# P turned inside one tile, six blocks moved, and the splits of P cut by key block

## The chip, the core and the metric

The kernel runs on one core of a Trainium2 chip. The metric is device time in microseconds of one execution. The core has TensorE (PE in the profile, with its weight loads as PEld), VectorE (DVE), ScalarE (ACT), GpSimd (POOL) and SyncE (SP, which here only issues DMAs; SPq is its queue, and ACTq is ScalarE's). Sixteen DMA engines move the data.

## What is computed

The reference, cut to what matters:

```python
x = x + einsum('bct,bcd->bdt', x, w0[idx])          # 32 batches, 128 x 1024, w0[idx] is 128 x 128
q, k, v = (einsum('bsd,ed->bse', x, W) for W in (Wq, Wk, Wv))   # 16 heads of 64
scores = einsum('bhqd,bhkd->bhqk', q * min(cond, 4), k) / sqrt(64)
scores = where(causal, scores, most negative)
attn = softmax(scores)                               # 128 queries x 128 keys per head
x = x + einsum('bsd,ed->bse', einsum('bhqk,bhkd->bhqd', attn, v), Wo)
```

All of it is float32. The kernel splits each operand of a product into a high half that TensorE takes in its fp32r form and a low half, the rest, and multiplies high by high, low by high and high by low into the same bank.

## The kernel before

The batches are taken in 8 groups of four. The program has three parts: the per-batch 128x128 product with the values projection (up to about 400 us), the attention with the q and k projections (400 to 1275 us), and the output projection (the first group in eight blocks inside the end of the attention part, the other 28 batches as 14 pairs behind it). The products of the values and of the pairs are seven block products in place of eight, with sums of blocks made on GpSimd.

The attention part is made of **cells**, numbered n = 0 to 63. One cell is four of the group's batches by two heads. In a cell TensorE runs eight steps of the q projection and eight of k (each step three 128x512 matmuls), the scores of an earlier cell (L710 to L712 into SC) and the values of a still earlier one. The written order is a table of times: each piece of work has a due time in units of TensorE steps, a cell is 16 of them, and each engine walks the times in quarter steps. A due time sets only the order on an engine; semaphores do the rest.

What happens to P, the softmax's numerator, in cell n (a is five steps behind the cell's key block):

- VectorE masks the scores (L1205) and takes row maxima (L1211), ScalarE makes the exponential with its row sums (L1035), VectorE the reciprocals (L1215), GpSimd the normalised P in two halves of 128x512 (L1333). PP holds it: query rows, then batch, head, key column.
- VectorE turns each 32x32 block of a half where it stands (L1102, `dve_turn`), into the tile TB, or WR from cell 58. The block of query block i and key block j then lies in the rows of i; TensorE needs it in the rows of j.
- SyncE moves the ten blocks of the lower triangle (L1530, `sp_move_p`), 32 rows by 256 elements each, from TB to the tile of P: PT in even cells, PT2 or xr[1] in odd ones. The masked blocks of these tiles are zeroed once.
- ScalarE makes the high half of two batches at a time (L1045), a 128x512 piece per half cell P = 2n + k, and GpSimd the low half (L1336). Both go to the tile PS, of which there is one.
- TensorE multiplies the values by PS: four matmuls 128x256 for each P (L815). Cell n's splits and values run while the projections of two cells later run. A values group waits for the low half of its own half cell.
- ScalarE and VectorE take the result from the two PV banks (L1052, L1053 into AC, and L1229 into AT), GpSimd adds them (L1339), SyncE stores (L1656).

Other work stands between: the splits of weight pieces in 48 of the cells (ScalarE L1012 or L1068, VectorE L1186 or L1235, SyncE's stores L1443 and L1445 or those of `sp_store_wo`), the splits of the group's values (L999, L1327), and in the last cells the split of the first output group's attention (Y: L1057 on ScalarE, L1343 on GpSimd).

Near the end of the attention SyncE's queue also has the loads of x1 for the eight output blocks (L1511), their stores (L1680), the loads of Wo (L1571; four further ones on ScalarE's queue, L965, behind the last splits of P), the loads of the first pairs' attention (L1586, which for the first pair wait for the last split of P) and those of the pairs' x1 (L1598, which wait for all eight output stores). VectorE gathers the pairs' products into x1 (L1261) and makes the low halves of their operands (L1239); GpSimd adds parts of the products to x1 (L1377) and makes the sums of blocks, the first of which is L1359.

## Time and profile before

| what | value |
|---|---|
| three runs | 1571.53, 1571.56, 1573.22 us (median 1571.56) |
| the profiled execution | 1573.44 us |
| its span, first to last instruction | 1572.10 us |
| PE busy | 1560.5 us (99%) |
| DVE, ACT, POOL busy | 980.2 (62%), 818.6 (52%), 856.7 us (54%) |
| mean granted TensorE clock | 0.999 |
| DMA traffic | 341.46 MB, mean 217 GB/s |
| GpSimd's low halves of P, L1336 | 128 of 128x512, 1293 ns each |
| ScalarE's high halves of P, L1045 | 128 of 128x512, about 620 ns each |
| moves of P, L1530 | 640 of 32 KB |

TensorE's busy time is near the span, so what the other engines do matters only where TensorE waits for it. A row of the waits says which engine waited, the tile and line it was about to work on, who released it, the total, how often, and the longest. A row of the timeline has the start, the time taken, the engine, its line, the operation with tiles, and in brackets the idle time before it.

### The profile page before, as it was taken

Reading aid. Unit: us, or ns where it says so; the run is one execution under the profiler, and the core shown is the slowest. Engines: PE = TensorE matmul, PEld = TensorE weight load, DVE = VectorE, ACT = ScalarE, POOL = GpSimd, SP = SyncE. Lnnn points to the kernel's source line nnn. Section 1 sums busy time; section 2 is a strip of 40 time slices with the busy share of each in tenths; the row PEclk is TensorE's granted clock in tenths of the full one; section 3 lists DMA queues with packets and bytes.
Section 4 is the critical chain, followed back from the end, with each engine's and each line's share of the span. In section 5 each row is a group of like instructions: output and inputs, shape, how many; then the busy total and the mean of one; then the engine's idle time right before and its main releaser. Section 6 shows DMA issues by size and latency. Waiting matters only on the chain.

```text
span 1572.1 us, 23424 instructions
## 1 busy us (share of the span) xinstructions
PE 1560.5 (99%) x7563; PEld 1311.5 (83%) x7563; DVE 980.2 (62%) x1748; ACT 818.6 (52%) x2221; POOL 856.7 (54%) x752
## 2 busy tenths in 40 slices
PE   9999999999999999999999999999999998999999
PEld 7888888888888888888888888888888876888887
DVE  5844454443367777777766777777777654555553
ACT  6645545543366666666666666666666621222220
POOL 1545645643255566557655566675577544555552
PEclk9999999999999999999999999999999999999999
DMA  9958888865866666767677466666665696444442
GB/s 325 338 209 276 306 285 296 300 218 217 304 184 193 208 204 201 209 193 193 184 241 235 154 176 209 192 189 194 192 180 154 232 353 240 167 161 164 164 162 86
DMA packets 192299, 341.46 MB, mean 217 GB/s; under 512 B 23986, under 2 KB 116402, under 8 KB 185010
## 3 DMA queue, kind: packets, MB, share of 16 engines
q1 hardware_dynamic: 191026, 331.59, 65.6%
q10 hardware_dynamic: 1152, 8.39, 1.3%
q8 instruction: 60, 0.98, 0.3%
q14 instruction: 61, 0.50, 0.1%
HBM read 184.70 MB, written 134.22 MB: 203 GB/s over the span
## 4 chain that ended last, share of the span: by engine, by line
PE 95%; DMA 3%; SPq 1%; POOL 0%; DVE 0%; issue 0%; ACT 0%; DVEq 0%; POOLq 0%; ACTq 0%
PE p_PJ L710 22%; PE p_PJ L711 22%; PE p_PJ L712 22%; PE p_SC L710 6%; PE p_SC L712 6%; PE p_SC L711 6%; PE p_PV L815 4%; PE p_PV L710 1%; PE p_PV L712 1%; PE p_PV L711 1%; DMA out<-t_LATE 1%; PE p_LP L710 1%; PE p_LP L712 1%; PE p_LP L711 1%; DMA t_LATE<-x_scratch 1%; PE p_PV L841 1%
## 5 line engine op out<-in xcount | busy, mean ns | idle before, releaser
L711 PE MATMUL p_PJ<-t_XL,t_WH 128*128 128x512 f32 x1008 | 394.1, 391 | 0.0
L710 PE MATMUL p_PJ<-t_XH,t_WH 128*128 128x512 f32 x1008 | 394.1, 391 | 0.0
L712 PE MATMUL p_PJ<-t_XH,t_WL 128*128 128x512 f32 x1008 | 392.1, 389 | 0.0
L1035 ACT ACTIVATE t_PP<-t_PP,t_st 128x128 f32<-128x128 f32 x512 | 199.5, 391 | 174.5 <-DVE t_st L1211 173.0
L1333 POOL TENSOR_TENSOR t_PP<-t_PP,t_st 128x512 f32<-128x512 f32 x128 | 133.4, 1042 | 204.9 <-DVE t_st L1215 204.9
L712 PEld LDWEIGHTS p_PJ<-t_XH,t_WL 128*128 128x128 f32 x1008 | 189.3, 188 | 40.4
L710 PEld LDWEIGHTS p_PJ<-t_XH,t_WH 128*128 128x128 f32 x1008 | 190.0, 189 | 33.8
L711 PEld LDWEIGHTS p_PJ<-t_XL,t_WH 128*128 128x128 f32 x1008 | 190.0, 188 | 32.3
L1229 DVE TENSOR_REDUCE t_AT<-p_PV 64x256 f32<-64x512 f32 x252 | 171.2, 680 | 20.8 <-ACT t_AC L1053 12.0
L1339 POOL TENSOR_TENSOR t_AT<-t_AT,t_AC 128x256 f32<-128x256 f32 x126 | 117.2, 930 | 122.7 <-DVE t_AT L1229 122.7
L1336 POOL TENSOR_TENSOR t_PS<-t_PT,t_PS 128x512 fp32r<-128x512 f32 x122 | 157.8, 1293 | 0.0
L1205 DVE SCALAR_TENSOR_TENSOR t_PP<-p_SC,t_beta,t_mask 128x256 f32<-128x256 f32 x256 | 111.6, 477 | 44.2 <-PE p_SC L712 44.2
L1322 POOL TENSOR_TENSOR t_xl<-t_XT,t_xh 128x512 fp32r<-128x512 f32 x56 | 74.0, 1321 | 94.9 <-ACT t_xh L917 94.2
L1215 DVE RECIPROCAL t_st<-t_st 128x4 f32<-128x4 f32 x128 | 22.9, 179 | 142.0 <-ACT t_PP L1035 142.0
L1022 ACT ACTIVATE t_KH<-p_PJ 64x512 fp32r<-64x512 f32 x128 | 76.1, 594 | 48.2 <-PE p_PJ L712 46.5
L1052 ACT ACTIVATE t_AC<-p_PV 64x256 f32<-64x256 f32 x128 | 48.9, 382 | 93.8 <-PE p_PV L815 92.3
L1035 ACT ACTIVATION_READ_ACCUMULATOR t_PP<-t_PP,t_st 128x1 f32 x512 | 95.6, 187 | 0.0
L1327 POOL TENSOR_TENSOR t_VV<-t_VX,t_VV 128x512 fp32r<-128x512 f32 x64 | 81.4, 1293 | 25.9 <-ACT t_VV L999 25.9
L1192 DVE TENSOR_TENSOR t_KL<-p_PJ,t_KH 64x512 fp32r<-64x512 f32 x128 | 88.2, 689 | 11.0 <-ACT t_KH L1022 7.1
L1211 DVE TENSOR_REDUCE t_st<-t_PP 128x2 f32<-128x256 f32 x256 | 94.1, 409 | 0.0
L815 PE MATMUL p_PV<-t_PS,t_VV 128*128 128x256 f32 x512 | 82.0, 283 | 1.2 <-POOL t_PS L1336 0.8
L815 PEld LDWEIGHTS p_PV<-t_PS,t_VV 128*128 128x128 f32 x512 | 74.2, 190 | 7.0 <-POOL t_PS L1336 1.2
(254 smaller groups left out, 3547.9 us busy)
## 6 DMA issues: line engine op xcount, KB each, us to landing
t_XH<-xth_scratch SPq DMA_DIRECT2D x56, 512.0 KB, 6.6
t_XL<-xtl_scratch SPq DMA_DIRECT2D x56, 512.0 KB, 7.0
t_PT<-t_TB SPq DMA_DIRECT2D x580, 32.0 KB, 2.4
v_scratch<-t_VR SPq DMA_DIRECT2D x64, 256.0 KB, 4.4
xth_scratch<-t_XH SPq DMA_DIRECT2D x16, 1024.0 KB, 4.0
xtl_scratch<-t_XL SPq DMA_DIRECT2D x16, 1024.0 KB, 6.3
t_VX<-v_scratch SPq DMA_DIRECT2D x32, 512.0 KB, 5.6
at_scratch<-t_AT SPq DMA_DIRECT2D x126, 128.0 KB, 3.4
```

What stands on the lines that cost most here:

```text
L710: pe.matmul(bank, lh, rh, start=first, stop=False, skip_group_check=goes_on)
L711: pe.matmul(bank, lh, rl, start=False, stop=False, skip_group_check=goes_on)
L712: return pe.matmul(bank, ll, rh, start=False, stop=last, skip_group_check=goes_on)
L815: mm = pe.matmul(PV2[:, z, 256 * h:256 * h + 256], VV[j % 2][:, u, 2 * c + h, :], moving, start=True, stop=True)
L1035: act.activation(PP[:, u, h, :], PP[:, u, h, :], ACT.Exp, bias=st[:, 0, u, h:h + 1], scale=1.0, accum_out=st[:, 1, u, h:h + 1]).then_inc(a ...
L1192: dve.tensor_tensor(KL[r, :, k], pj[r], KH[r, :, k].bitcast(f32), ALU.subtract).then_inc(dve_k, 1)
L1205: dve.scalar_tensor_tensor(out=PP[:, u], in0=SC[u // 2][:, 256 * (u % 2):256 * (u % 2) + 256].rearrange("p (h k) -> p h k", h=2), scalar=b ...
L1211: dve.tensor_reduce(st[:, 0, u, :], PP[:, u], AX, ALU.max, negate=True).then_inc(dve_m, 1)
L1229: dve.tensor_reduce(at_tile(P)[r], both, AX, ALU.add).then_inc(dve_M, 1)
L1333: pool.tensor_tensor(pp, pp, r, ALU.mult).then_inc(pool_n, 1)
L1336: pool.tensor_tensor(p_half(P, 1), p_raw(P), p_half(P, 0).bitcast(f32), ALU.subtract).then_inc(pool_pt, 1)
L1339: pool.tensor_tensor(at_tile(P), at_tile(P), AC[:, P % 2], ALU.add).then_inc(pool_at, 1)
```

## The change

Turned blocks are written straight into the tile of P (TB or PT2 before cell 58, PT or WR from there). The four blocks on the diagonal are then in their place already. Six DMAs move the others, from the lower to the upper triangle of the same tile. Each parity of cells has its own semaphore for them. What the moves leave behind in the lower triangle is no longer zero, so the splits read, for key blocks of one query block i, only the rows up to 32i + 31: four splits per cell and engine, each of all eight batch-heads of the cell, on 32, 64, 96 and 128 rows with 256 elements in a row. The rows that they never write are zero in PS, which is filled once instead of the tiles of P. The due times of the splits and of the moves change, and the values groups wait for all four splits of their cell.

```diff
-                move_at.put(a + 10, n)
+                move_at.put(a + 10.5, n)
...
-                    half_at.put(a + (20 if last else 25.25) + 0.5 * k, P)
-                    ptl_at.put(a + (20.75 if last else 26) + 1.5 * k, P)
+                    if k == 0:
+                        half_at.put(a + (18 if last else 22.25), n)
+                        ptl_at.put(a + (18.75 if last else 23.25), n)
...
-        def turned(n):
-
-            return TB[:] if n < 58 else WR[:].rearrange("p a (b c) -> p (a b) c", b=2).rearrange("p j (u q) -> p j u q", u=8)
-
         def p_tile(n):
 
-            return PT if n % 2 == 0 else PT2 if n < 58 else xr[1][:].rearrange("p (i q) -> p i q", i=4)
+
+            if n < 58:
+                return TB[:] if n % 2 == 0 else PT2[:].rearrange("p j (u q) -> p j u q", u=8)
+            if n % 2 == 0:
+                return PT[:].rearrange("p j (u q) -> p j u q", u=8)
+            return WR[:].rearrange("p a (b c) -> p (a b) c", b=2).rearrange("p j (u q) -> p j u q", u=8)
...
-        def p_half(P, low):
-
-            u = 4 * (P % 2)
-            return PS[:, u:u + 4, low, :].rearrange("p u (i q) -> p u i q", i=4)
-
-        def p_raw(P):
-            u = 4 * (P % 2)
-            return p_tile(P // 2)[:].rearrange("p i (u q) -> p u i q", u=8)[:, u:u + 4]
+        def p_half(i, low):
+
+            return PS[0:32 * i + 32, :, low, 32 * i:32 * i + 32]
+
+        def p_raw(n, i):
+            return p_tile(n)[0:32 * i + 32, i]
...
-                pe.wait_ge(pool_pt, P + 1)
+                pe.wait_ge(pool_pt, 4 * n + 4)
...
-                for P in half_at(tick):
-                    n = P // 2
-                    act.wait_ge(l_P, 160 * (n + 1))
+                for n in half_at(tick):
+                    act.wait_ge(l_P[n % 2], 96 * (n // 2 + 1))
+                    act.wait_ge(dve_t, 2 * n + 2)
                     if n:
                         act.wait_ge(pe_pv, 4 * n)
-                    act.activation(p_half(P, 0), p_raw(P), ACT.Copy).then_inc(act_pt, 1)
+                    else:
+                        act.wait_ge(pool_z, 4)
+                    for i in range(4):
+                        act.activation(p_half(i, 0), p_raw(n, i), ACT.Copy).then_inc(act_pt, 1)
...
-            elif n == 58:
-                dve.wait_ge(s_O, 32 * 32)
-            elif k == 0:
-                dve.wait_ge(l_P, 160 * n)
+            elif n >= 2 and k == 0:
+
+                dve.wait_ge(pool_pt, 4 * (n - 1))
...
-                    pool.memset(PT[:], 0.0).then_inc(pool_z, 1)
-                    pool.wait_ge(dve_g, 5 * (NP - 2))
-                    pool.memset(PT2[:], 0.0).then_inc(pool_z, 1)
-                if tick == (T_END - 76) * TICK:
-                    pool.wait_ge(dve_O, 32)
-                    pool.memset(xr[1][:], 0.0).then_inc(pool_z, 1)
+                    pool.memset(PS[:].bitcast(f32), 0.0).then_inc(pool_z, 1)
...
-                for P in ptl_at(tick):
-                    pool.wait_ge(act_pt, P + 1)
-                    pool.tensor_tensor(p_half(P, 1), p_raw(P), p_half(P, 0).bitcast(f32), ALU.subtract).then_inc(pool_pt, 1)
+                for n in ptl_at(tick):
+                    for i in range(4):
+                        pool.wait_ge(act_pt, 4 * n + i + 1)
+                        pool.tensor_tensor(p_half(i, 1), p_raw(n, i), p_half(i, 0).bitcast(f32), ALU.subtract).then_inc(pool_pt, 1)
...
             sp.wait_ge(dve_t, 2 * n + 2)
-            if n == 0:
-                sp.wait_ge(pool_z, 5)
-            elif n >= 2:
-                sp.wait_ge(pool_pt, 2 * n - 2)
-            if n == 59:
-                sp.wait_ge(pool_z, 6)
+            tile = p_tile(n).rearrange("p j u q -> p j (u q)")
             for i in range(4):
-                for j in range(i + 1):
-                    src = turned(n)[32 * i:32 * i + 32, j].rearrange("a u q -> a (u q)")
-                    sp.dma_start(p_tile(n)[32 * j:32 * j + 32, i, :], src).then_inc(l_P, 16)
+                for j in range(i):
+                    sp.dma_start(tile[32 * j:32 * j + 32, i], tile[32 * i:32 * i + 32, j]).then_inc(l_P[n % 2], 16)
```

Waits elsewhere that counted the half cells' splits (the loads of Wo and of the first pair, the first sum of a pair) count the new ones to the same point.

How it moves the order on three queues. First GpSimd, in one cell of the middle of the attention, from its two normalising operations (t_PP) on; t_PS are the splits, t_AT the sums, t_VV the split of values. Before:

```order
L1333 TENSOR_TENSOR t_PP<-t_PP,t_st 128x512 x2
L1336 TENSOR_TENSOR t_PS<-t_PT,t_PS 128x4x128
L1339 TENSOR_TENSOR t_AT<-t_AT,t_AC 128x256
L1336 TENSOR_TENSOR t_PS<-t_PT,t_PS 128x4x128
L1327 TENSOR_TENSOR t_VV<-t_VX,t_VV 128x4x128 x2
L1339 TENSOR_TENSOR t_AT<-t_AT,t_AC 128x256
```

And with the change, in the same cell:

```order
L1331 TENSOR_TENSOR t_PP<-t_PP,t_st 128x512 x2
L1335 TENSOR_TENSOR t_PS<-t_PT,t_PS 32x8x32
L1335 TENSOR_TENSOR t_PS<-t_PT,t_PS 64x8x32
L1335 TENSOR_TENSOR t_PS<-t_PT,t_PS 96x8x32
L1335 TENSOR_TENSOR t_PS<-t_PT,t_PS 128x8x32
L1338 TENSOR_TENSOR t_AT<-t_AT,t_AC 128x256
L1325 TENSOR_TENSOR t_VV<-t_VX,t_VV 128x4x128 x2
L1338 TENSOR_TENSOR t_AT<-t_AT,t_AC 128x256
```

The second split of a cell stood behind a sum of AT; all four now stand ahead of it.

Next SyncE's queue in an early cell that also splits a weight piece; t_VX is the load of values, t_OH and t_OL the halves of the weight piece. Before:

```order
L1656 DMA at_scratch<-t_AT 128x256
L1499 DMA t_VX<-v_scratch 128x1024 x2
L1530 DMA t_PT<-t_TB 32x256 x10
L1443 DMA wh_scratch<-t_OH 512x1x128
L1445 DMA wl_scratch<-t_OL 512x1x128
L1656 DMA at_scratch<-t_AT 128x256
```

With the change:

```order
L1649 DMA at_scratch<-t_AT 128x256
L1498 DMA t_VX<-v_scratch 128x1024 x2
L1442 DMA wh_scratch<-t_OH 512x1x128
L1444 DMA wl_scratch<-t_OL 512x1x128
L1523 DMA t_TB<-t_TB 32x256 x6
L1649 DMA at_scratch<-t_AT 128x256
```

The two stores of the weight piece's halves stand ahead of the moves now.

Last, SyncE's queue around the last cell's moves; t_LATE and t_xr hold x1 and the output. Before:

```order
L1571 DMA t_WL<-wol_scratch 128x2048
L1511 DMA t_LATE<-x_scratch 128x512
L1511 DMA t_xr<-x_scratch 128x512
L1530 DMA t_xr<-t_WR 32x256 x10
L1680 DMA out<-t_xr 128x512
L1656 DMA at_scratch<-t_AT 128x256
L1511 DMA t_xr<-x_scratch 128x512
```

With the change:

```order
L1564 DMA t_WL<-wol_scratch 128x2048
L1510 DMA t_LATE<-x_scratch 128x512
L1510 DMA t_xr<-x_scratch 128x512
L1523 DMA t_WR<-t_WR 32x256 x6
L1673 DMA out<-t_xr 128x512
L1649 DMA at_scratch<-t_AT 128x256
L1510 DMA t_xr<-x_scratch 128x512
```

The order stays; six DMAs stand where ten stood.

## Rows read from the trace of the kernel before

**Rows 1.** Windows: stretch, its length, each engine busy (instructions), clock, DMA share, GB/s.

```profile
420.00:740.00 320.00, 320.00 (x1631) 273.52 (x1630) 233.83 (x474) 205.83 (x644) 188.17 (x169) 1.00 0.69 200
```

**Rows 2.** Waits of PE from 1240 to 1345: total, times, longest.

```profile
PE p_SC L710 <- DVE t_xr L1261: 2.0, 1, 2.0
PE p_SC L710 <- issue: 1.8, 1, 1.8
PE p_SC L710 <- DVE t_XL L1239: 1.0, 1, 1.0
```

**Rows 3.** Windows, two of 2 us behind the last of these waits.

```profile
1317.00:1319.00 2.00, 2.00 (x7) 1.58 (x8) 0.46 (x1) 0.00 (x0) 1.05 (x1) 0.72 0.69 258
1319.00:1321.00 2.00, 2.00 (x6) 1.59 (x5) 0.00 (x0) 0.00 (x0) 1.50 (x2) 0.50 0.10 35
```

**Rows 4.** Timeline of an ordinary cell: start, time taken, engine, line, operation.

```profile
870.46 1.14 ACT L1045 ACTIVATE t_PS<-t_PT 128x512 fp32r<-128x512 f32 x2
...
871.37 1.30 POOL L1336 TENSOR_TENSOR t_PS<-t_PT,t_PS 128x512 fp32r<-128x512 f32 x1
...
873.86 0.73 POOL L1339 TENSOR_TENSOR t_AT<-t_AT,t_AC 128x256 f32<-128x256 f32 x1 [1.20 <-DVE t_AT L1229]
...
874.28 0.65 PEld L815 LDWEIGHTS p_PV<-t_PS,t_VV 128*128 128x128 f32 x4
874.51 0.64 PE L815 MATMUL p_PV<-t_PS,t_VV 128*128 128x256 f32 x4
874.56 1.28 POOL L1336 TENSOR_TENSOR t_PS<-t_PT,t_PS 128x512 fp32r<-128x512 f32 x1
```

**Rows 5.** Timeline of the last ordinary cell, n = 61.

```profile
1244.52 1.30 POOL L1336 TENSOR_TENSOR t_PS<-t_xr,t_PS 128x512 fp32r<-128x512 f32 x1
...
1247.43 0.65 PEld L815 LDWEIGHTS p_PV<-t_PS,t_VV 128*128 128x128 f32 x4
```

**Rows 6.** Timeline of a cell with the split of a weight piece.

```profile
604.83 1.30 POOL L1336 TENSOR_TENSOR t_PS<-t_PT,t_PS 128x512 fp32r<-128x512 f32 x1
...
607.28 0.69 DVE L1186 TENSOR_TENSOR t_OL<-t_xr,t_OH 128x512 fp32r<-128x512 f32 x1
607.33 1.24 POOL L1339 TENSOR_TENSOR t_AT<-t_AT,t_AC 128x256 f32<-128x256 f32 x1 [1.20 <-DVE t_AT L1229]
```

**Rows 7.** Timelines of POOL and DVE where the pairs' operands begin.

```profile
1281.38 1.30 POOL L1359 TENSOR_TENSOR t_WR<-t_PP,t_PT 128x512 f32<-128x512 f32 x1 [5.10 <-DMA t_PT<-at_scratch]
...
1282.00 1.23 DVE L1239 TENSOR_TENSOR t_VL<-t_PP,t_VH 128x512 fp32r<-128x512 f32 x1 [3.41 <-ACT t_VH L1080]
```

**Rows 8.** Timeline of SyncE's queue at the last cell's moves: time taken is that of issue.

```profile
1259.28 6.24 SPq L1530 DMA_DIRECT2D t_xr<-t_WR  x10
1265.57 0.58 SPq L1680 DMA_DIRECT2D out<-t_xr  x1
...
1273.67 0.38 SPq L1586 DMA_DIRECT2D t_PP<-at_scratch  x1
```

**Rows 9.** Page, DMA issues: count, KB each, median us from issue to landing.

```profile
t_PT<-t_TB SPq DMA_DIRECT2D x580, 32.0 KB, 2.4
```

**Rows 10.** Timelines of POOL and PEld in cell 59.

```profile
1218.37 1.29 POOL L1336 TENSOR_TENSOR t_PS<-t_xr,t_PS 128x512 fp32r<-128x512 f32 x1
...
1220.78 0.65 PEld L815 LDWEIGHTS p_PV<-t_PS,t_VV 128*128 128x128 f32 x4
```

**Rows 11.** Windows around the end of the attention; the last two numbers are DMA share and GB/s.

```profile
1266.00:1270.00 4.00, 4.00 (x19) 3.30 (x19) 1.28 (x3) 1.15 (x2) 0.00 (x0) 1.00 0.55 154
...
1274.00:1302.00 28.00, 27.65 (x124) 22.70 (x123) 14.51 (x18) 8.71 (x17) 12.10 (x9) 1.00 1.04 402
```

**Rows 12.** The chain that ended last, from 1240 to 1345: start, time taken, what.

```profile
1284.43 15.57 DMA t_LATE<-x_scratch
...
1316.17 0.70 DVE t_xr L1261
```

**Rows 13.** Timeline of PE at the last cell's first values.

```profile
1272.45 0.74 PE L815 MATMUL p_PV<-t_PS,t_VV 128*128 128x256 f32 x4 [0.81 <-POOL t_PS L1336]
```

More of the change, by code:

```diff
@@ L206, in cond_attention @@
         pool_n, dve_t = sem("normed"), sem("p_turned")
-        act_pt, pool_pt, l_P = sem("pt_high"), sem("pt_low"), sem("load_pt")
+        act_pt, pool_pt, l_P = sem("pt_high"), sem("pt_low"), [sem(f"move_p{n}") for n in range(2)]
         act_c, dve_M, pool_at = sem("at_other_rows"), sem("at_own_rows"), sem("at_out")
@@ L1562, in sp_load_wo @@
                 sp.wait_ge(s_O, 32 * 32)
[L1564 removed]
+                sp.wait_ge(pool_pt, 4 * 58)
             elif k == 3:
@@ L1575, in sp_load_pair @@
             if q == 0:
-                sp.wait_ge(pool_pt, 2 * 64)
+                sp.wait_ge(pool_pt, 4 * 64)
             elif q == 1:
```

5 lines of the change are left out of this document (2 added, 3 removed).

## The prediction

> **What bounds the kernel now.** I read the windows first. In the attention part TensorE is busy 320.00 of 320.00 us at full clock [rows 1], so neither the four DMAs fewer nor a cheaper split can save anything there: only a new wait of TensorE counts, and it counts once per cell, some 60 times. The waits of TensorE come next: of its idle time three pieces lie in one stretch of 15 us at the first product behind the attention, 2.0, 1.8 and 1.0 us, 4.8 together [rows 2]. So two places decide: the distance in each cell from the splits of P to the values matmuls, and what feeds that first product.
>
> The measure: the span is 1572.10 us, the profiled execution took 1573.44, so 1.34 lie around the span. The three runs gave 1571.53, 1571.56 and 1573.22. In the profiled one the granted clock fell to 0.72 and 0.50, the lower level of 1.2 GHz, right behind the longest of these waits [rows 3]; over the two windows that costs 2 x (0.28 + 0.50) = 1.6 us. 1573.44 less 1.6 is 1571.8, near the two lower runs: I take the median as a run without that fall and subtract from 1571.56. The profiled time would move by as much.
>
> **The cell: what is added.** Per cell ScalarE's splits go from two of 128x512 to four with 256 elements in each row, on 32, 64, 96 and 128 rows, and GpSimd's likewise. Values now wait for all four, where the first pair waited for the first of two. In an ordinary cell GpSimd begins its first split at 871.37, right behind the second normalising op, and TensorE loads the first weights of values at 874.28 [rows 4]: 2.91 us. So it is in 60 of the 64 cells, in the last of them from 1244.52 to 1247.43 [rows 5]; cell 0 has more, cells 59, 62 and 63 have less. GpSimd still splits right behind its two normalising ops, so the start stays.
>
> How long the four take: no op of that shape is in the trace. The nearest is the sum of AT, 256 elements a row, same engine and operation: 0.73 us, with the next op 0.70 behind its start (873.86 to 874.56) [rows 4]. From below, half of a present split is 0.65; for the end above I keep 0.77, because there the trouble of the next part starts. I take 0.70, since operation, operands and elements a row are the same: 3 x 0.70 + 0.73 = 2.83, done at 874.20, 0.08 us ahead of the weight load. Fewer rows are priced like 128, as no row shows a gain by that. So the cover in each cell is 0.08 us; when it is gone, TensorE pays what is missing, each time.
>
> ScalarE isn't in the way: its splits start at 870.46 [rows 4]; even if each of the four took the 0.62 of today's, the last would be done at 872.9, and GpSimd reaches its fourth at 873.47. Behind them on ScalarE stands the key copy, which waits for TensorE's next block anyway.
>
> **The cell: the port.** In 48 of the 64 cells VectorE also takes the low half of a weight piece (L1186, L1235), with both operands in SBUF. In such a cell it starts at 607.28, and the sum of AT that GpSimd starts at 607.33 takes 1.24 us in place of 0.73 [rows 6]: GpSimd is held off until VectorE is through. Counted from the first split (604.83) VectorE comes at 2.45; the fourth split would run from 2.10 to 2.83, right across. What happens when GpSimd is first shows in the tail: its sum from 1281.38 takes its normal 1.30, and VectorE, which comes at 1282.00, takes 1.23 [rows 7], where the same operation takes 0.69 in [rows 6]. So the fourth split keeps its length, and VectorE's op ends 0.55 behind it, at 3.4 in place of 3.14. The two key splits behind it, as long each, then end at 4.8, and TensorE needs them for the scores, three steps of projections behind the values, at about 5.6. Cost zero.
>
> By the Trainium skill (SBUF — State Buffer, the section on which engines share ports) a VectorE instruction with two SBUF inputs and a GpSimd one that reads SBUF exclude each other for a whole instruction, and the one that starts first wins. By that rule the sum stays; by a rule that VectorE always wins, the fourth split would end some 0.7 us later and the kernel would take about 1598. The trace agrees with the first.
>
> **The cell: the moves.** Ten moves take 6.24 us to issue [rows 8], six 3.7, so SyncE gains 2.5 us in each cell. In the 48 cells the two stores of the halves now stand ahead of the moves and wait for VectorE's op: the moves start at about 3.4 + 1.2 and have been issued at 8.3 us behind the first split. A cell is 13.33 us, (1244.52 - 871.37) / 28; ScalarE reads them one cell later, at 12.4: 4.1 us for a landing that takes 2.4 in the median [rows 9]. No cost. 8 MB less go through the DMA engines, off the path. One zeroing of PS ahead of the attention takes the place of three of P's tiles, while GpSimd is idle. VectorE's turns keep shape and number and wait for less.
>
> **Cell 59.** Here GpSimd comes late from a low half of Y: its first split starts at 1218.37, and values load at 1220.78 [rows 10], 2.41 us later. Four splits end at 1221.20, so TensorE stands 0.42 us, and all that follows with it. Cell 62 has a like stall, but the chain of the tail doesn't pass through it.
>
> **The tail: what is removed.** The chain of waits leads back from the last gather for that product, at 1316.17, to the loads of x1 and from these, load by store, over SyncE's queue to the moves of the last cell: issued from 1259.28 for 6.24 us, with the next store of output right behind them at 1265.57 [rows 8]. Six moves in place of ten: 4 x 0.62 = 2.5 us earlier. Less the 0.42 of cell 59, SyncE is 2.1 us earlier. The splits of the last cell start 2 us earlier too, the weight loads on ScalarE's queue with them, and the load of Y for the first pair, which waits for the last split until 1273.67 [rows 8], comes some 4 us earlier. TensorE's wait for the last splits ends; it is inside what follows.
>
> Does what starts earlier end earlier? From 1274 to 1302 the DMA engines are full; from 1266 to 1270 they are at 0.55 [rows 11]. One load takes 15.57 us in that jam [rows 12]. A jam with the same bytes that starts 2.1 us earlier ends 2.1 earlier, and the gap at 0.55 can be filled: 4 x 0.45 = 1.8 us at most; I take 0.2 of it. Behind the jam come the loads for the pair, sums, and the gather at 1316.17 [rows 12], all unchanged. So the product starts 2.3 us earlier, and TensorE has 4.8 us of idle to give up for it. The rest is TensorE's own work: 1571.56 - 2.3 = **1569.3 us**. Late next is still that chain, with some 2.5 us of idle left.
>
> **The rivals.**
> (a) More comes forward. The whole gap is filled, 2.1 + 1.8 = 3.9, or all 4.8 us of idle go: 1567.7 to 1566.8. For it: the load of Y comes 4 us earlier. Against: ScalarE's loads come earlier as well and share the engines with the chain.
> (b) The tail doesn't move: the loads that come forward displace the store chain by as much as it gained. 1571.6, and nothing for cell 59, which then lies inside TensorE's idle time.
> (c) The cover of 0.08 us is not enough. Behind its wait in the last cell TensorE's values took 0.74 [rows 13] in place of 0.64 [rows 4]: a release so close may cost up to 0.1 us in 60 cells, 6 us. Splits of 0.74 in place of 0.70 would be done at 2.99, 0.08 too late, 4.8 us. Times from 1569.3 to 1580, the middle 1574.5. For it: a wait met 0.08 us ahead is not one met long ago. Against: that row follows a long idle time.
> (d) **The port is lost**, the rival on the other side. The place is the fourth split in the 48 cells. GpSimd needs the port some 0.13 us behind its start (in [rows 6] the overlap is 0.64 us, the delay 0.51). If splits follow each other by over 0.77 us, the fourth starts at 2.31 and comes behind VectorE's 2.45. Then it ends at 3.14 + 0.60 = 3.74, TensorE loses 3.74 - 2.91 = 0.83 us, 48 times, 40 us, and 0.2 in 12 others: 1569.3 + 42 = 1611. For it: [rows 6] shows the loss itself. Against: a margin of 0.2 us, and [rows 7].
> (e) That the change doesn't do what it says: six moves end no sooner if SyncE first waits for something else. In the last cell nothing stands ahead of them, so this would be (b).
>
> **How the numbers follow.** Forecast 0.46, own range 1567.8 to 1571; (a) 0.14; (b) 0.10; (c) 0.18; (d) 0.12. About 0.2%, 3.1 us, is what a measurement of this kernel can tell from no change: faster is below 1568.4, slower above 1574.7. Faster: 0.07 of the forecast and (a), 0.21. Same: 0.39, (b) and half of (c), 0.58. Slower: half of (c) and (d), 0.21. The range leaves out (d) and the upper third of (c): 1566.5 to 1577.
>
> **What will show it.** Right: windows of the attention with TensorE busy all the time and cells of 13.33 us, GpSimd's splits 0.70 apart, VectorE's low halves at about 1 us and not 0.69, the output store behind the last moves near 1263.4, the last gather near 1313.9. (b) would show as the same 1306 for the pair's loads, (c) as a short wait for t_PS in each cell, (d) as a fourth split of 1.4 us behind VectorE's low half. A cell longer than 13.33 us makes the prediction wrong.

## The result, and the profile after

| what | before | after |
|---|---|---|
| median, lowest to highest, runs | 1572.24 us, 1571.53 to 1573.22, 4 | 1586.18 us, 1584.79 to 1587.81, 4 |
| ratio, 95% interval | | 1.009, 1.0078 to 1.0102 |
| profiled execution, its span | 1573.44, 1572.10 us | 1586.54, 1585.2 us |
| DVE busy | 980.2 us | 1024.1 us |

The change makes the kernel slower by 14 us, 0.9%. The forecast was 1569.3 us, its range 1566.5 to 1577.

The windows of the attention part hide it. The row that answers to [rows 1], with the same columns, still shows TensorE busy for 320.00 of 320.00 us:

```profile
420.00:740.00 320.00, 320.00 (x1603) 264.71 (x1602) 249.77 (x464) 203.18 (x668) 177.92 (x211) 1.00 0.61 187
```

In the same time TensorE did 1603 matmuls where it did 1631. A matmul's end is modelled in the profile, and the waits of its weights are not shown as idle time of TensorE here, so a busy share of 100% says nothing about waits of 0.3 us. The count of instructions does, and so does PEld, the weight load, which fell from 273.52 to 264.71. Before, neither PE nor PEld has a wait from 430 to 1240. After, the waits of PEld in that stretch are (in total, times, longest):

```profile
PEld p_PV L816 <- POOL t_PS L1335: 15.8, 49, 0.5
PEld p_SC L711 <- DVE t_KL L1195: 14.0, 46, 0.3
```

Laid over each other by the start of the values matmuls, the two traces part in the two stretches of cells in which a weight piece is split: 46 cells take 13.633 us, where before all took 13.327, 0.306 us more, and the four at the ends of the stretches 0.05 to 0.12 more. That is 14.4 us, 0.30 for each of the 48 splits. From cell 28 to cell 35, which have no such split, the distance stays the same to 0.001 us. With 0.35 us that is lost in cell 59, the attention part is 14.75 us behind at cell 61. The timeline of one of the slow cells (cell 20), GpSimd first, then VectorE (start, time taken, engine, line):

```profile
704.43 2.81 POOL L1335 TENSOR_TENSOR t_PS<-t_TB,t_PS 32x256 fp32r<-32x256 f32 x4
707.22 0.72 POOL L1338 TENSOR_TENSOR t_AT<-t_AT,t_AC 128x256 f32<-128x256 f32 x1
```

```profile
706.88 1.60 DVE L1238 TENSOR_TENSOR t_OL<-t_xr,t_OH 128x512 fp32r<-128x512 f32 x1
708.52 1.41 DVE L1195 TENSOR_TENSOR t_KL<-p_PJ,t_KH 64x512 fp32r<-64x512 f32 x2
709.96 1.41 DVE L1232 TENSOR_REDUCE t_AT<-p_PV 64x256 f32<-64x512 f32 x2
711.41 0.88 DVE L1208 SCALAR_TENSOR_TENSOR t_PP<-p_SC,t_beta,t_mask 128x256 f32<-128x256 f32 x2
```

The four splits take 2.81 us, as forecast. VectorE's low half of the weight piece (L1238) comes at 2.45 behind the first of them, as forecast. But it takes 1.60 us and not 0.95: it doesn't end 0.55 behind the fourth split (707.24), but 0.54 behind the sum of AT (707.94). VectorE waited for the rest of one GpSimd operation and for the whole of the next. Key splits, own sums and masks follow without a gap.

The same stretch of VectorE before, cell 20 too:

```profile
700.57 0.69 DVE L1235 TENSOR_TENSOR t_OL<-t_xr,t_OH 128x512 fp32r<-128x512 f32 x1
701.29 1.41 DVE L1192 TENSOR_TENSOR t_KL<-p_PJ,t_KH 64x512 fp32r<-64x512 f32 x2
702.75 1.41 DVE L1229 TENSOR_REDUCE t_AT<-p_PV 64x256 f32<-64x512 f32 x2
704.78 0.48 DVE L1205 SCALAR_TENSOR_TENSOR t_PP<-p_SC,t_beta,t_mask 128x256 f32<-128x256 f32 x1 [0.62 <-PE p_SC L712]
```

The last row has the number that the prediction lacked: ahead of the masks VectorE waited 0.62 us for the scores. It is all that VectorE had to spare. The waits of DVE from 430 to 800, of before and of after, say the same as a total:

```profile
DVE t_PP L1205 <- PE p_SC L712: 17.5, 28, 0.6
```

```profile
DVE t_PP L1208 <- PE p_SC L713: 0.6, 1, 0.6
```

So the first theory: the low half takes 0.91 us more, 0.62 of it goes into this wait, and 0.29 is lost in each of the 48 cells, 14 us. Behind the masks nothing takes the delay up: VectorE's waits for the exponentials are 0.90 and 1.36 us before and after alike. Exponential, reciprocal, normalising and turn follow from the masks and lead back to VectorE's next cell, so the delay goes round this ring with every cell, and TensorE, held back at two places, is only a part of it.

At the end of the attention the changed kernel wins something. SyncE's queue after, to be read beside [rows 8]:

```profile
1274.52 3.69 SPq L1523 DMA_DIRECT2D t_WR<-t_WR  x6
1278.26 0.58 SPq L1673 DMA_DIRECT2D out<-t_xr  x1
...
1282.15 0.32 SPq L1510 DMA_DIRECT2D t_xr<-x_scratch  x1
```

The moves take 3.69 us in place of 6.24, and the store is issued 2.55 us earlier behind their start. From the first values matmul of cell 61 to the first matmul behind TensorE's last long wait, in the pair's first product, it is 67.3 us after and 69.4 before; the fall of the granted clock behind that wait [rows 3] is in both and lasts 3.41 us in both.

### The profile page after: what moved, and what is told of

It reads as the page before. It is cut to its first block, busy times and chain, and to the rows that moved or that the text cites. A ratio compares the mean times of both kernels' runs of the same rounds, so it can differ in the third digit from the quotient of the medians.

```text
span 1585.2 us, 23295 instructions
## 1 busy us (share of the span) xinstructions
PE 1574.3 (99%) x7563; PEld 1303.3 (82%) x7563; DVE 1024.1 (65%) x1748; ACT 829.4 (52%) x2349; POOL 846.3 (53%) x878
## 4 chain that ended last, share of the span: by engine, by line
PE 96%; POOL 1%; DMA 1%; DVE 0%; issue 0%; ACT 0%; SPq 0%; ACTq 0%; DVEq 0%; POOLq 0%
PE p_PJ L711 22%; PE p_PJ L712 22%; PE p_PJ L713 22%; PE p_SC L711 6%; PE p_SC L712 6%; PE p_SC L713 6%; PE p_PV L816 4%; PE p_PV L711 1%; PE p_PV L713 1%; PE p_PV L712 1%; PE p_LP L711 1%; PE p_LP L712 1%; PE p_LP L713 1%; PE p_PV L842 1%; PE p_LP L842 1%; DMA out<-t_LATE 1%
## 5 line engine op out<-in xcount | busy, mean ns | idle before, releaser
L1338 POOL TENSOR_TENSOR t_AT<-t_AT,t_AC 128x256 f32<-128x256 f32 x126 | 92.0, 730 | 108.8 <-DVE t_AT L1232 108.8
L1208 DVE SCALAR_TENSOR_TENSOR t_PP<-p_SC,t_beta,t_mask 128x256 f32<-128x256 f32 x256 | 111.7, 478 | 16.0 <-PE p_SC L713 14.4
L1335 POOL TENSOR_TENSOR t_PS<-t_PT,t_PS 32x256 fp32r<-32x256 f32 (+3 forms) x128 | 90.2, 728 | 0.0
L816 PE MATMUL p_PV<-t_PS,t_VV 128*128 128x256 f32 x512 | 87.0, 292 | 0.6 <-DVE t_LATE L1232 0.3
L816 PEld LDWEIGHTS p_PV<-t_PS,t_VV 128*128 128x128 f32 x512 | 70.4, 189 | 18.3 <-POOL t_PS L1335 16.4
```

The costliest lines, as they stand in the source:

```text
L816: mm = pe.matmul(PV2[:, z, 256 * h:256 * h + 256], VV[j % 2][:, u, 2 * c + h, :], moving, start=True, stop=True)
L1208: dve.scalar_tensor_tensor(out=PP[:, u], in0=SC[u // 2][:, 256 * (u % 2):256 * (u % 2) + 256].rearrange("p (h k) -> p h k", h=2), scalar=b ...
L1335: pool.tensor_tensor(p_half(i, 1), p_raw(n, i), p_half(i, 0).bitcast(f32), ALU.subtract).then_inc(pool_pt, 1)
L1338: pool.tensor_tensor(at_tile(P), at_tile(P), AC[:, P % 2], ALU.add).then_inc(pool_at, 1)
```

## The experiments

All distances within a cell are measured from the start of GpSimd's first split in a cell, those of the tail from the first values matmul of cell 61. The span of the profiled execution is given where there was one run only; that of before stands at 1572.1, and 1.3 us lie around it. "Passed over" means below that VectorE waits while GpSimd starts its next operation; "served", that VectorE gets its turn and GpSimd's next operation is held off.

### Is it this one instruction?

In `e1_low_behind_keys` VectorE's loop for the low halves stands behind the key splits:

```diff
+            p_low.put(quiet(m - 14) + 2.5, m)
+                O_low.put(O_cell(8 * c + k) + 2.5, (c, k))
...
-                for m in p_split(tick - TICK):
+                for m in p_low(tick):
...
-                for c, k in O_split(tick - TICK):
+                for c, k in O_low(tick):
```

> The changed kernel, with one thing moved: in the 48 cells with the split of a weight piece, VectorE's low half of the piece stands behind the two key splits and no longer ahead of them, and SyncE's two stores of the halves follow it. So it would start at 3.9 us behind GpSimd's first split of P, when GpSimd's sum of AT (2.78 to 3.51) is done. Theory: the 0.306 us that each of these cells takes more (13.633 for 13.327) come from this one instruction, which took 1.60 us in place of 0.69 because it came across the fourth split. Then it takes 0.69 here, the cells are 13.327 again, TensorE's waits for the key halves (14.0 us) and for the splits of P (15.8 us) go, and the time is about 1570: 1586.2 less 14.75, less what the tail shows. Rival: the cells are longer because four splits in a row put the values 0.05 us behind the last of them; then moving the low half changes nothing, 1586. Rival: the low half only meets GpSimd elsewhere; between 1570 and 1586.

Measured: 1572.21 us median of 11 runs (1570.39 to 1572.51), before 1572.03 of 27 runs, ratio 1.0, 0.9991 to 1.0009. The cells are 13.327 again; cell 23, VectorE:

```profile
741.11 1.41 DVE L1194 TENSOR_TENSOR t_KL<-p_PJ,t_KH 64x512 fp32r<-64x512 f32 x2
742.55 0.69 DVE L1241 TENSOR_TENSOR t_OL<-t_xr,t_OH 128x512 fp32r<-128x512 f32 x1
743.29 1.41 DVE L1235 TENSOR_REDUCE t_AT<-p_PV 64x256 f32<-64x512 f32 x2
745.32 0.88 DVE L1211 SCALAR_TENSOR_TENSOR t_PP<-p_SC,t_beta,t_mask 128x256 f32<-128x256 f32 x2 [0.62 <-PE p_SC L716]
```

The low half has its 0.69 back, and the 0.62 of waiting stand ahead of the masks again. The wait for the key halves is gone, that for the splits of P is down to 0.9 us. The loss hangs on this one instruction. But 1570 wasn't reached: no gain from the tail can be told from no change.

### Late keys or late masks?

Two places of TensorE wait in the changed kernel, and both could be the cause. `e2_more_work_behind_keys` is e1 with as much more work for VectorE as the changed kernel's wait takes. It stands behind the keys, ahead of each low half:

```diff
+            for part in [512, 4]:
+                ...
+                dve.tensor_tensor(low[:, :part], raw[:, :part], high[:, :part], ALU.subtract).then_inc(dve_again, 1)
```

> The kernel of e1_low_behind_keys with more work for VectorE: behind the key splits of each of the 48 cells the low half is made twice (0.69 us more) and four of its columns a third time (about 0.2), so that VectorE has the same 0.9 us more as in the changed kernel, but with the key halves on time and without GpSimd in the way. What is left out of the question: the output is the reference's. Theory (the masks are late): VectorE had only 0.62 us to spare ahead of the masks of the scores (the wait for the scores in a cell of the kernel before); what goes beyond that is lost in each cell, 0.27 to 0.3 us, 48 times, so 13 to 15 us more than e1_low_behind_keys. Rival (the keys are late): TensorE's 14.0 us of waits for the key halves are the loss; here they don't come up, and the time is that of e1_low_behind_keys.

Measured: 1586.75 us median of 4 (1585.26 to 1588.67), ratio 1.0091, 1.0075 to 1.0106. The cells take 13.642 us. VectorE in one of them:

```profile
734.41 1.41 DVE L1206 TENSOR_TENSOR t_KL<-p_PJ,t_KH 64x512 fp32r<-64x512 f32 x2
735.86 0.89 DVE L1158 TENSOR_TENSOR t_OL<-t_xr,t_OH 128x512 fp32r<-128x512 f32 x2
736.78 0.69 DVE L1256 TENSOR_TENSOR t_OL<-t_xr,t_OH 128x512 fp32r<-128x512 f32 x1
737.51 1.41 DVE L1249 TENSOR_REDUCE t_AT<-p_PV 64x256 f32<-64x512 f32 x2
738.95 0.88 DVE L1225 SCALAR_TENSOR_TENSOR t_PP<-p_SC,t_beta,t_mask 128x256 f32<-128x256 f32 x2
```

The keys are on time, no wait for them is in the trace, the splits aren't disturbed, and the loss is the same: 0.92 us more, less 0.62, is 0.30, and 0.315 was measured. Late keys are not needed for the loss; late masks are enough. VectorE's own sums are late here too, but they stand ahead of the 0.62 us of waiting, and in e3 below they are 0.24 us late at no cost. TensorE's wait for the keys is only where it shows.

### Does a pause of GpSimd let VectorE in?

`e3_sum_waits` leaves the order of the changed kernel as it is and adds a wait ahead of GpSimd's sum, on the semaphore of the low half of that cell:

```diff
                     pool.wait_ge(dve_M, 2 * P + 2)
+                    if P % 2 and P // 2 in low_cells:
+                        at, m = low_cells[P // 2]
+                        pool.wait_ge(at, m)
```

> The changed kernel, with one wait added: in the 48 cells GpSimd's sum of AT behind the four splits of P waits until VectorE has made the low half of the weight piece. Theory: VectorE, which comes at 2.45 us during the fourth split, doesn't get its turn between two GpSimd instructions that stand back to back, only when GpSimd pauses. With the pause it starts its 0.55 us of work at the end of the fourth split (2.82) and ends at 3.4, so it takes 0.95 and not 1.60; 0.26 more than in the kernel before is less than the 0.62 to spare ahead of the masks, the cells are 13.327 again, and the time is about 1570. Rival: the low half is slow for another reason (the reading of P's tiles by three engines, the DMAs): it stays at 1.60, and the time at 1586 or above.

Measured: 1571.93 us median of 10 (1570.51 to 1573.71), ratio 0.9998, 0.9989 to 1.0007. GpSimd and VectorE:

```profile
753.35 1.43 POOL L1341 TENSOR_TENSOR t_PS<-t_TB,t_PS 96x256 fp32r<-96x256 f32 x2
755.47 0.74 POOL L1347 TENSOR_TENSOR t_AT<-t_AT,t_AC 128x256 f32<-128x256 f32 x1 [0.70 <-DVE t_OL L1244]
```

```profile
754.40 0.93 DVE L1244 TENSOR_TENSOR t_OL<-t_xr,t_OH 128x512 fp32r<-128x512 f32 x1
```

0.93 us, 0.55 behind the end of the fourth split (754.78): just what the prediction had (0.95). With that the low half is 0.24 longer than before, less than the 0.62 to spare, and costs nothing. So the prediction's idea of one collision was right, and the sum behind the split made the loss.

### Which ends of a GpSimd operation let VectorE in?

Whether two splits and the sum in a row are enough, `e4_before_sum_behind` asked of the kernel before:

```diff
-                    ptl_at.put(a + (20.75 if last else 26) + 1.5 * k, P)
+                    ptl_at.put(a + (20.75 if last else 26) + (1.5 if last else 1) * k, P)
```

> The kernel before, with one thing changed in the order: GpSimd's second split of P stands ahead of the sum of AT, not behind it (its due time is half a step earlier). Two splits of 1.3 and the sum then follow each other without a pause: 0 to 1.3, 1.3 to 2.55, 2.55 to 3.3. Theory: VectorE's low half comes at 2.45, is passed over once by the sum, and ends at 3.3 + 0.55, about 3.85: 1.4 us in place of 0.69. That is 0.7 more, 0.08 beyond what VectorE has to spare: 48 times, 4 us, about 1576. Rival (VectorE gets its turn at the end of the second split): 0.69 + 0.1, no change of the time, 1572. Rival (the loss needs the four narrow splits): 0.69, 1572.

Measured: 1572.53 us median of 10, ratio 1.0001, 0.9991 to 1.001. My 1576 was wrong. The second split ended 0.09 us behind the start of the low half, which took 0.69 in nearly all cells, and the sum behind it was held off to 1.24. An operation so near its end doesn't hold VectorE off. In two cells of the trace the split ended 0.29 and 0.68 behind the start; there the low half took 0.84 and 1.23, and the sum waited. That spoke against "passed over by whatever follows", so I looked further, one execution each. `e6_one_more_behind_sum` puts an added operation (256 elements a row, float32) behind the sum of the changed kernel, `e7_before_more_ahead` one ahead of the splits of e4:

```diff
+                        pool.tensor_tensor(JK[:], *pair, ALU.add).then_inc(pool_j, 1)
```

> The changed kernel with one more GpSimd operation (256 elements a row, its result unused) directly behind the sum of AT that follows the four splits; VectorE's low half is back ahead of the key splits. If VectorE gets no turn as long as GpSimd's instructions stand back to back, the low half ends 0.55 us behind the added one: some 2.2 us in place of 1.60; the cells with it are 0.9 us longer than 13.327 and not 0.306, and the time is about 1613. If it is passed over once only, it stays near 1.6, with the added operation held off, and the time near 1586.

> The kernel before with its second split ahead of the sum of AT, as in e4_before_sum_behind, and one GpSimd operation of 256 elements a row (its result unused) ahead of the two splits of each cell. In e4 the second split ended 0.09 us behind VectorE's start, and VectorE's low half took its 0.69 as ever, with the sum held off to 1.24. Here the split ends some 0.6 us behind VectorE's start, so VectorE is really waiting when the sum follows without a pause. If a waiting VectorE is passed over by the next GpSimd instruction whatever the shapes, the low half takes 0.6 + 0.7 + 0.55 = 1.85 us, the cells with it are 13.327 + 1.85 - 0.69 - 0.62, about 13.87, and the time about 1598. If VectorE gets its turn at the end of the split, it takes 1.15 us, the sum behind it is held off, and the time stays at 1572: then the loss belongs to the narrow splits alone.

Spans: 1617.8 us (e6) and 1571.0 (e7). In e6 the low half waits for both, and the cells take 14.334 us. GpSimd, then VectorE:

```profile
733.43 1.43 POOL L1337 TENSOR_TENSOR t_PS<-t_PT,t_PS 96x256 fp32r<-96x256 f32 x2
734.82 0.72 POOL L1340 TENSOR_TENSOR t_AT<-t_AT,t_AC 128x256 f32<-128x256 f32 x1
735.51 0.72 POOL L1345 TENSOR_TENSOR t_JK<-t_mask,t_ident 128x256 f32<-128x256 f32 x1
```

```profile
734.47 2.31 DVE L1240 TENSOR_TENSOR t_OL<-t_xr,t_OH 128x512 fp32r<-128x512 f32 x1
```

In e7 VectorE waits 0.79 us of the wide split and gets its turn at its end; it is the sum that is held off, to 1.19:

```profile
686.53 2.54 POOL L1343 TENSOR_TENSOR t_PS<-t_PT,t_PS 128x512 fp32r<-128x512 f32 x2
689.03 1.19 POOL L1346 TENSOR_TENSOR t_AT<-t_AT,t_AC 128x256 f32<-128x256 f32 x1
```

```profile
688.27 1.34 DVE L1237 TENSOR_TENSOR t_OL<-t_xr,t_OH 128x512 fp32r<-128x512 f32 x1
```

The next ones put added operations between others: two of 256 elements with a 16-bit result behind the first split of the kernel before (`e9_narrow_ones_in_before`), one of 512 elements with a 16-bit result behind the four splits (`e10_wide_one_behind_splits`).

> The kernel before with two GpSimd operations of 256 elements a row (results unused) between the first split of P (512 elements) and the sum of AT (256), which the second split (512) follows. All of them stand back to back; VectorE's low half comes at 2.45 us, during the second added one. So far: a waiting VectorE got its turn at the end of a GpSimd operation of 1.3 us (e7: 1.34 us, the sum behind it held off to 1.19), and was passed over at the end of one of 0.73 (the changed kernel: 1.60; e6: 2.31, passed over twice). If the length of the operation that ends decides, and not that the splits are narrow in rows or that the kernel is the changed one, VectorE is passed over at the end of the second added one, and of the sum, and gets its turn behind the second split: 4.7 + 0.55 - 2.45, about 2.8 us. If it is only passed over by short ones, the second split lets it through: about 1.5 us. If it is served at once, 0.8.

> The changed kernel with one more GpSimd operation of 512 elements a row (result unused) between the fourth split of P (256) and the sum of AT (256), back to back. VectorE's low half comes at 2.45 us, during the fourth split. If the length of the operation that ends decides, VectorE is passed over at 2.82 and gets its turn at the end of the long one: 4.1 + 0.55 - 2.45, about 2.2 us, with the sum of AT held off. If all are passed over until GpSimd pauses, 2.9 us; if the long one lets it through at 2.82, 0.93.

e9: 0.79 us in the mean, span 1571.8. The second added operation ends 0.24 us behind VectorE's start and VectorE is served there, so the length alone isn't what decides. e10: 2.21, span 1614.6. VectorE is passed over at the end of the fourth split and served at the end of the added one, with the sum held off:

```profile
703.03 1.42 POOL L1337 TENSOR_TENSOR t_PS<-t_PT,t_PS 96x256 fp32r<-96x256 f32 x2
704.42 1.28 POOL L1344 TENSOR_TENSOR t_JK<-t_mask,t_ident 128x512 bf16<-128x512 f32 x1
705.67 1.23 POOL L1346 TENSOR_TENSOR t_AT<-t_AT,t_AC 128x256 f32<-128x256 f32 x1
```

```profile
704.09 2.21 DVE L1240 TENSOR_TENSOR t_OL<-t_xr,t_OH 128x512 fp32r<-128x512 f32 x1
```

Four more, each with one added operation of 256 elements: `e12_sum_ends_in_before` ahead of the sum in the kernel before; `e13_half_type_behind_splits` and `e14_full_type_behind_splits` between the fourth split and the sum of the changed kernel, with a 16-bit and a float32 result; `e15_other_behind_wide` behind the wide split of e7.

> The kernel before with one GpSimd operation of 256 float32 elements a row (result unused) between the first split of P and the sum of AT, so that VectorE's low half, at 2.45 us, comes during the sum (1.97 to 2.7), which the second split of P (512 elements) follows without a pause. In e6 the sum was passed over from, in e10 and e9 an added operation with a 16-bit result of 512 or 256 elements let VectorE through. If the end of a sum (256 elements, float32) is what lets GpSimd go on, VectorE is passed over here too and takes 3.97 + 0.55 - 2.45, about 2.1 us; if passing over belongs to the changed kernel's narrow splits only, it takes 0.8 us.

> The changed kernel with one GpSimd operation of 256 elements a row and a 16-bit result between the fourth split of P and the sum of AT. VectorE is passed over at the end of the fourth split as in the changed kernel. If the 16-bit operation lets it through (as in e9), the low half takes 1.60 us and the sum of AT behind it is held off to 1.2; if not, 2.3 us with the sum at its 0.73.

> The same as e13_half_type_behind_splits, but with a float32 result: the operation between the fourth split and the sum. If the type or the form of the operation that ends decides, this one doesn't let VectorE through where e13's does: 2.3 us and a sum at 0.73 (passed over twice), as in e6. If it lets it through as well, 1.60 us and a sum of 1.2, the form doesn't decide but the place: the first end behind VectorE's arrival is lost, the second isn't, and e6's second loss stays unexplained.

> The kernel of e7_before_more_ahead with one more GpSimd operation of 256 float32 elements a row (result unused) between the second split of P (512 elements) and the sum of AT. In e7 the end of this split let VectorE through, with the sum behind it. If the operation that ends decides, it lets VectorE through here too: 1.34 us, and the added operation is held off to 1.2. If the one that follows decides (in e6 an added operation went ahead of VectorE where in e7 a sum did not), VectorE is passed over here and gets its turn behind the added one: about 2.0 us.

e12 told nothing: the sum waits for VectorE's own sums and can't start before 2.5, so no GpSimd operation ran when the low half came, and it took 0.69. e13 and e14: 1.69 and 1.66 us in the mean, spans 1589.0 and 1586.3; in nearly all cells VectorE is passed over at the fourth split and served at the end of the added operation, whatever its type (in e13 the first cell of each of the two stretches is passed over twice, 2.31). e15: 1.34 us, span 1573.2; the wide split lets VectorE in with another operation behind it too:

```profile
769.36 1.19 POOL L1352 TENSOR_TENSOR t_JK<-t_mask,t_ident 128x256 f32<-128x256 f32 x1
```

| GpSimd operation that ends while VectorE waits | what follows at once | VectorE |
|---|---|---|
| fourth split, 256 elements a row | sum (after, e6), added one of 256 (e13, e14) or of 512 (e10) | passed over |
| sum of AT, 256 elements, float32 | added one (e6) | passed over |
| second split of before, 512 elements | sum (e7, two cells of e4), added one (e15) | served |
| added one, 256 or 512 elements | sum (e9, e10, e14, and e13 but for two cells) | served |

But for the two cells of e13, the outcome goes with the operation that ends, not with the one that follows. Why the short operations on the kernel's own tiles let GpSimd go on, and the added ones on two small tables (read over again for each 128 elements) do not, stays open: these runs change length, type, operands and alignment together, and only one of them has the sum as the one that ends. What does hold in all of them is the price. The cell grows by what the low half takes beyond 0.69 + 0.62 us:

| kernel | low half, mean us | less 1.31 | cell less 13.327 |
|---|---|---|---|
| e9 | 0.79 | none | 0.00 |
| e3 | 0.93 | none | 0.00 |
| e7 | 1.33 | 0.02 | 0.02 |
| e15 | 1.34 | 0.03 | 0.03 |
| after | 1.60 | 0.29 | 0.306 |
| e14 | 1.66 | 0.35 | 0.364 |
| e13 | 1.69 | 0.38 | 0.36 |
| e10 | 2.21 | 0.90 | 0.91 |
| e6 | 2.31 | 1.00 | 1.01 |

### Where the gain of the tail went

`e5_ten_in_last_cell` takes e1 and issues four DMAs more in the last cell, and so undoes only the SyncE part of the tail's gain:

```diff
+                if n == 63:
+                    sp.dma_start(diag_d[i], tile[32 * i:32 * i + 32, i]).then_inc(s_diag, 16)
```

> The kernel of e1_low_behind_keys with ten DMAs in the last cell in place of six: four stores of the diagonal blocks, 32 KB each, to memory that nobody reads, stand between the moves. The output store behind them is then issued 2.5 us later, as in the kernel before (14.8 us behind the first values of cell 61, where the changed kernel has 12.2). Theory (the DMA engines are full at that time): the store issued at 12.2 lands only 4.6 us later, since from 8 to 18 us the engines are full (shares 0.98 to 1.06); one issued at 14.8 takes about 2.5, so the next load of x1 goes out 0.5 us later and the last gather for the pairs' first product comes 0.2 to 1 us later. Rival (what starts earlier ends earlier, as predicted): the store lands 4.6 us behind its issue again, and all that follows comes 2.5 us later.

Measured: span 1571.2 us. The store behind the moves and the load of x1 that waits for its landing, in e1 first, then in e5:

```profile
1260.21 3.68 SPq L1526 DMA_DIRECT2D t_WR<-t_WR  x6
1263.93 0.58 SPq L1676 DMA_DIRECT2D out<-t_xr  x1
...
1268.56 0.32 SPq L1513 DMA_DIRECT2D t_xr<-x_scratch  x1
```

```profile
1266.06 0.42 SPq L1680 DMA_DIRECT2D out<-t_xr  x1
...
1268.91 0.32 SPq L1515 DMA_DIRECT2D t_xr<-x_scratch  x1
```

The two runs reach cell 61 within 0.02 us of each other. Issued 2.1 us earlier, the store lets the load go 0.35 us earlier: it took 4.6 us in place of 2.8. The pair's first product starts 0.95 us earlier. The window of the kernel before over that stretch, which I had not read (I began at 1266, [rows 11]), says why:

```profile
1256.00:1266.00 10.00, 10.00 (x49) 8.44 (x48) 5.27 (x9) 3.73 (x13) 6.04 (x6) 1.00 0.90 310
```

The DMA engines are at 0.90 there, mostly with the loads of Wo and x1 issued just ahead. The store goes out earlier into a jam that ends when it ends. Over all profiles in which no other load is moved, the x1 loads of the first pair are issued 56.3 to 57.2 us behind cell 61's first values in eight kernels with six moves (after, e1, e2, e3, e6, e10, e13, e14) and 57.5 to 58.4 in seven with ten (before, e4, e5, e7, e9, e12, e15): 56.7 and 57.8 in the mean, 1.1 us for four DMAs fewer. The pair's first product starts at 67.8 and 68.9 in the mean, 1.1 us apart as well.

Two tries to get more out of it, both on e1. `e8_weights_behind_store` takes a pair of 1 MB loads out of the jam, `e11_later_weights` one from ahead of the last load of x1:

```diff
-        for k, high, low in (... (2, 9.5, 9.5), ... (4, 50, 50), ...):
+        for k, high, low in (... (2, 16, 16), ... (4, 50, 50), ...):     # e8
+        for k, high, low in (... (2, 9.5, 9.5), ... (4, 54, 54), ...):   # e11
```

> The kernel of e1_low_behind_keys with one pair of loads moved on SyncE's queue: the high and low half of Wo's third quarter (1 MB each), which stand ahead of the last cell's moves, stand behind them and behind the output store. Theory (the moves and the store stand in the jam that these 2 MB make): without it the store lands some 2.5 us behind its issue and not 4.6, the next load of x1 goes out at about 15 and not 16.8 us behind the first values of cell 61, the 2 MB fill the 2 to 4 us in which the engines are at 0.2 to 0.5, and the last gather comes 1 to 2 us earlier: 1570.5 to 1571.5 where e1 has 1572.2. Rival (all of the bytes have to pass, the order doesn't matter): no change, 1572. Rival: the eighth-to-last block waits for these weights, slower by 1 to 2 us.

> The kernel of e1_low_behind_keys with one pair of loads (the fifth part of Wo, 2 x 1 MB) 4 steps of TensorE later on ScalarE's queue. In e1 these 2 MB are issued 3 us ahead of the last load of x1 for the output blocks, which then takes 15.0 us to land, and TensorE's product of the first pair waits behind it. Theory: behind the load of x1 the 2 MB don't hold it up; the last output block is ready when TensorE has made it, 2 to 3 us earlier, its store takes longer in turn (8.3 us in place of 5.7), and the last gather comes 0.5 to 1 us earlier: 1571.5 where e1 has 1572.2. Rival: the same bytes end at the same time, no change. Rival: the product waits for these weights itself: slower by 1 us.

e8: 1574.26 us median of 11 (1572.78 to 1576.97), ratio 1.0016, 1.0007 to 1.0025, slower. The store did land in 2.9 us and the load went out at 18.2 in place of 20.0 us. But the stores of AT stand behind the 2 MB now, and the waits of PE from 1200 to 1345 have a new row:

```profile
PE p_PV L819 <- DVE t_AT L1235: 6.3, 1, 6.3
```

One wait took the place of another. In and behind this one the granted clock was at 0.50 for 6.83 us, which is a part of the loss too. e11: 1572.08 us median of 11, ratio 0.9996, 0.9987 to 1.0005: no change that can be measured. No version here beats the kernel before.

## Why the prediction was wrong

**The splits and their cover: right.** Four splits take 2.81 to 2.83 us against the 2.83 of the sum, the cover held in all ordinary cells (0.09 to 0.11 us in cells 28 to 34, 0.08 predicted), and ScalarE was early enough. Rival (c) didn't come up. Rival (d) didn't either: the fourth split took 0.73 in each cell and was never held off by VectorE. The moves were never late in the attention.

**The port in the 48 cells: the step that failed.** The prediction had "VectorE's op ends 0.55 behind it, at 3.4 in place of 3.14 [...] Cost zero". Two things were wrong with it. First the size: it ended at 4.05, since the sum of AT stood right behind the fourth split and went first. The order of the change, which I had shown in front of the prediction, has that sum there; I used [rows 6] and [rows 7], where one GpSimd operation and one of VectorE's meet, and didn't ask what VectorE does when two GpSimd operations follow each other. The GpSimd operation in [rows 7] is also of 512 elements a row, and in e7 and e15 it is behind such a one that VectorE is served. Second the cover: I compared the end of the key splits only with TensorE's need for them, about 5.6 against 4.8. VectorE's own queue goes on behind them with two sums and the masks, and its slack was the 0.62 us ahead of the masks, not the 0.8 that seemed to be left. With the size right and this cover, the sum would have been 0.91 - 0.62 = 0.29, 48 times, 14 us: 1583, near what came. With the size as predicted (e3) the cost is zero indeed. So the size decided, and the wrong cover kept me from seeing how close it was.

By the Trainium skill (SBUF — State Buffer, the section SBUF: two separate sides) the one of the two that starts first has the shared ports for its whole instruction, and the other waits. For one collision the runs agree (e3: 0.93 us, 0.55 behind the split's end). Who has them next when GpSimd's operations follow each other goes beyond that rule: e6 shows VectorE waiting for three in a row, 2.31 us, and e7 shows it served at the first end.

**Cell 59: right.** GpSimd's first split at 1233.25, the values' weights at 1236.12; this stall cost 0.35 us (0.42 predicted). Another 0.19 us was lost once in cells 14 and 15 in e1 and e3 alike, where GpSimd came late; the prediction had not looked for it.

**The tail: the mechanism was right, the term too large.** Six moves made the store's issue 2.55 us earlier (2.5 predicted), but the pair's loads come only 1.1 us earlier than with ten, where the sum had 2.7 ahead of the loss in cell 59. The step that failed is "A jam with the same bytes that starts 2.1 us earlier ends 2.1 earlier". The store didn't start the jam; it stood in an earlier one, from 1256 to 1266, that was there in any case. With 1.1 - 0.35 - 0.19, the rest is about 0.6 us, less than can be told from no change, and e1 and e3 show just that: with this term put right and without the fault in the cells the sum would have been 1571, close to rival (b) at 1571.6.

**The measure.** The prediction put the difference between the two runs at 1571.5 and the one at 1573.2 down to the fall of the granted clock [rows 3], and took the lower ones as runs without it. The price holds, the reading of the lower runs isn't shown. The clock is at 0.50 for 3.41 us in this stretch in 14 of the 17 profiles. In seven (before, after, e2, e9, e10, e11, e15) that comes behind TensorE's last long wait. In seven others (e1, e4, e5, e7, e12, e13, e14) it comes one wait earlier, as here in e1, a window and then the waits of PE behind it:

```profile
1313.00:1315.00 2.00, 2.00 (x7) 1.52 (x5) 1.08 (x1) 0.53 (x1) 2.00 (x2) 0.50 1.02 359
PE p_SC L714 <- DVE t_xr L1267: 0.4, 1, 0.4
```

The twelve matmuls between the two waits are slower then, 3.6 to 4.2 us from the first to the last in place of 2.6, and the last wait is 0.4 to 0.8 us in place of 2.0: it takes the cost up. From the matmul behind the last wait to the end of the span it is 255.0 to 255.1 us in the first seven and 253.4 to 253.5 in the second, and the same 253.4 to 253.5 in e3 and e6, which have no fall here. So 1.6 us hang on where the fall comes. It also means that one run against one run says nothing below 0.2%: 27 runs of the kernel before went from 1570.8 to 1573.6.

## What to carry to other kernels

Where an operation may be held off on one engine, follow that engine's own queue to its next wait: the slack is the idle time printed in front of the next instruction that waits, not the distance to the consumer that comes to mind. Look at what stands directly behind the operation that holds it off: here a second short one went first too, and a wait that makes the other engine pause gave back all that was lost in the cells. And a busy share of 100% with fewer instructions of the same work in the same window hid a stall.

## What I hadn't expected of the hardware

- A VectorE operation with both operands in SBUF that waits for GpSimd is not always served when the GpSimd operation ends. With GpSimd's instructions back to back it was passed over by one (1.60 us in place of 0.93 to 0.95) or two (2.31 us); behind other operations it was served at once (1.34 us, of them 0.79 for the rest of a split of 1.29, the next GpSimd operation held off from 0.73 to 1.19).
- An operation with 0.09 us to go doesn't hold VectorE off at all (0.69 us in e4).
- TensorE's granted clock fell to 0.50 at the end of or behind a wait of 1.9 to 2.9 us in 14 of 17 profiles, for 3.41 us in each, and for 6.83 us from within e8's wait of 6.3 us on. In e3 and e6 it didn't, with waits of 1.5 to 2.1 us, nor behind e9's wait of 3.0 us, but behind its next one of 2.0. The fall cost 1.6 us of 1572 where no wait came behind it, more than the change gains in the tail, and nothing where the next wait took it up. What decides whether and where it comes stays open.
- TensorE shown as busy for 320.00 of 320.00 us had lost 0.3 us in each of 20 cells.
